# Landing numbers read ahead, and running counts per tile of tokens: one change to a fused attention and expert kernel

## The reference, cut to what matters

```python
logits = flat @ router_w.T
probs = jax.nn.softmax(logits.astype(jnp.float32), axis=-1)
topk_p, topk_i = jax.lax.top_k(probs, TOP_K)          # TOP_K = 2
topk_w = topk_p / jnp.maximum(topk_p.sum(-1, keepdims=True), 1e-09)
combine = combine.at[jnp.arange(T)[:, None], topk_i].add(topk_w)
for e in range(E):
    out = out + _mlp(flat, w_fc[e], w_proj[e]) * combine[:, e:e + 1]
out = out + _mlp(flat, shared_fc, shared_proj)
...
x = _layernorm(x + _L0_ffn_ref(x, ...), axis=-1)
```

## Time and profile before

| what | us |
|---|---|
| median of 3 runs (480.43 to 483.86) | 480.66 |
| the profiled execution | 480.25 |
| its span, first to last instruction | 478.4 |
| TensorE matmul busy | 443.9 (93%) |
| VectorE busy | 356.6 (75%) |
| ScalarE busy | 354.9 (74%) |
| GpSimd busy | 318.1 (66%) |

### The profile page before, as it was taken

The page is one execution under the profiler, slowest core; times in us unless marked ns, Lnnn a source line. Parts: engine busy times, 40 slices in busy tenths (PEclk is TensorE's granted clock), DMA queues, the critical chain, the costliest instruction groups (busy, mean ns, idle before and its releaser), DMA issues.

```text
span 478.4 us, 7874 instructions
## 1 busy us (share of the span) xinstructions
PE 443.9 (93%) x2193; PEld 288.9 (60%) x2193; DVE 356.6 (75%) x870; ACT 354.9 (74%) x557; POOL 318.1 (66%) x294
## 2 busy tenths in 40 slices
PE   8997999999999998877889988999999999999973
PEld 5343444444344333334666766789999999999821
DVE  5889999999999999999888977453333333555465
ACT  3989999999999999952675555556666666666655
POOL 4763788888898989881677667734555545655541
PEclk9998999999999999999999999999999999999999
DMA  8032226673434343200111111142223221222457
GB/s 284 11 93 84 78 73 214 217 245 136 157 136 159 136 157 136 92 1 1 47 45 52 50 41 52 55 111 59 69 68 85 67 65 53 62 70 66 147 176 220
DMA packets 41196, 48.68 MB, mean 102 GB/s; under 512 B 5616, under 2 KB 25266, under 8 KB 41152
## 3 DMA queue, kind: packets, MB, share of 16 engines
q1 hardware_dynamic: 35792, 39.16, 25.0%
q0 software_dynamic: 5216, 8.70, 6.0%
q10 hardware_dynamic: 144, 0.31, 0.3%
HBM read 19.26 MB, written 29.11 MB: 101 GB/s over the span
## 4 chain that ended last, share of the span: by engine, by line
PE 43%; POOL 22%; DVE 17%; issue 8%; ACT 6%; SPq 2%; DMA 2%; POOLq 0%; DVEq 0%; ACTq 0%
POOL memory_feat L505 17%; PE routed_ph L1591 13%; PE routed_po L1606 13%; PE dispatch_spo L1074 3%; PE dispatch_sph L1064 3%; DVE memory_y_raw L788 2%; POOL memory_feat L513 2%; DVE memory_prod L779 2%; POOL memory_prod L528 2%; PE routed_px L1579 2%; PE memory_nsum L630 2%; SPq L1737 1%; DVE memory_feat L779 1%; PE memory_ph L636 1%; DVE dispatch_stats L1319 1%
## 5 line engine op out<-in xcount | busy, mean ns | idle before, releaser
L505 POOL TENSOR_TENSOR memory_feat<-memory_feat,memory_p_tok 128x1024 f32<-128x1024 f32 x64 | 125.9, 2063 | 17.1 <-ACT memory_feat L400 14.2
L630 PE MATMUL memory_nsum<-memory_feat,tri 128*128 128x512 f32 x256 | 116.8, 598 | 6.3 <-ACT memory_last_rows L413 2.4
L1567 POOL DMA_INDIRECT pick_scratch<-routed_ob,routed_xg x71 | 72.1, 1016 | 65.2 <-DVE routed_ob L1689 52.0
L630 PEld LDWEIGHTS memory_nsum<-memory_feat,tri 128*128 128x128 f32 x256 | 47.6, 191 | 64.4 <-issue 54.6
L1274 POOL DMA_INDIRECT table_scratch<-dispatch_xrow,dispatch_slot x64 | 62.3, 973 | 30.3 <-issue 14.4
L1639 ACT ACTIVATE routed_rel<-routed_ph 128x512 f32<-128x512 f32 x71 | 42.3, 597 | 45.0 <-PE routed_ph L1591 45.0
L1689 DVE TENSOR_SCALAR routed_ob<-routed_po,routed_xg 128x128 f32<-128x128 f32 x71 | 22.6, 348 | 67.2 <-PE routed_po L1606 67.1
L1606 PE MATMUL routed_po<-routed_w2c,routed_hid 128*128 128x128 f32 x568 | 71.1, 275 | 0.5 <-ACT routed_hid L1648 0.5
L1591 PE MATMUL routed_ph<-routed_xs,routed_w1c 128*128 128x256 f32 (+1 forms) x368 | 71.2, 337 | 0.0
L779 DVE TENSOR_TENSOR memory_prod<-memory_nsum,memory_query 128x1024 f32<-128x1024 f32 x58 | 68.8, 1216 | 2.0 <-PE memory_nsum L630 1.8
L1606 PEld LDWEIGHTS routed_po<-routed_w2c,routed_hid 128*128 128x128 f32 x568 | 67.0, 192 | 0.8 <-ACT routed_hid L1648 0.7
(11 more groups left out here) (202 smaller groups left out, 695.6 us busy)
## 6 DMA issues: line engine op xcount, KB each, us to landing
table_scratch<-memory_blank SPq DMA_DIRECT2D x68, 260.0 KB, 2.6
dispatch_xrow<-pick_scratch SPq DMA_DIRECT2D x16, 256.0 KB, 3.1
routed_xg<-table_scratch SPq DMA_DIRECT2D x25, 130.0 KB, 2.2
w<-w_up SPq DMA_DIRECT2D x9, 256.0 KB, 2.7
w<-w_down SPq DMA_DIRECT2D x9, 256.0 KB, 3.2
x_tok<-x SPq DMA_DIRECT2D x4, 512.0 KB, 3.7
out<-x_tok SPq DMA_DIRECT2D x7, 256.0 KB, 4.1
routed_xg<-table_scratch SPq DMA_DIRECT2D x21, 65.0 KB, 1.9
```

Of the source, the lines that this page charges most:

```text
L505: nc.gpsimd.tensor_tensor(v, v, pv, ALU.mult).then_inc(wfeat_done, 1)
L630: last = nc.tensor.matmul(nsum[:, o:o + 512], tri[:], feat[:, i % U, h, q * 512:(q + 1) * 512], start=True, stop=True)
L1567: nc.gpsimd.indirect_dma_start(out=pick_dram, in_=ob[:, u, h, :], in_offset=None, out_offset=bass.IndirectOffsetOnAxis(ap=xg[:, t % XU, h, ...
```

## The change: what it does

Three edits. First, the reads of the landing numbers move: SP's routed loop reads the four numbers of group `t - 10` behind the load of tile `t`, for tiles 10 to 17, keeps all 32 in registers and hands them to the finish; the wait for `settled` moves with them, into tile 10. Second, `count` no longer reduces a group to one sum. It runs behind `choose` and in front of `place`, and adds the four tiles of `sel` one after another, so that `seen` holds the counts ahead of each of the 32 tiles; VectorE waits for the last of them. Third, `rank` makes two products, the triangular one and one with ones on the four rows of `seen`; it waits for its own group's count, where before it needed only the count of the group before. `totals` takes every fourth row of `seen`.

```diff
-        self.part = sb("part", [P, E])
-        self.seen = sb("seen", [P, NG + 1, E], F32R)
+        self.seen = sb("seen", [P, NT + 1, E], F32R)
...
             def rank(g):
                 pe.wait_ge(sel_done, g + 1)
-                pe.wait_ge(seen_done, g + 1)
+                pe.wait_ge(seen_done, g + 2)
                 pe.wait_ge(log_kept, g + 1)
-                sv = sel[:, g % 2].rearrange("p t e -> p (t e)")
-                nc.tensor.matmul(pr[:, 0:GT * E], tri_r[:], sv, start=True, stop=False)
-                for t in range(GT - 1):
-                    nc.tensor.matmul(pr[:, (t + 1) * E:GT * E], ones_r[:],
-                                     sel[:, g % 2, t:t + 1, :].broadcast_to([P, GT - 1 - t, E]), start=False, stop=False)
-                nc.tensor.matmul(pr[:, 0:GT * E], ones_r[:],
-                                 seen[:, g].unsqueeze(1).broadcast_to([P, GT, E]), start=False, stop=True
+                nc.tensor.matmul(pr, tri_r[:], sel[:, g % 2].rearrange("p t e -> p (t e)"), start=True, stop=False)
+                nc.tensor.matmul(pr, ones_r[:], seen[:, group(g), :].rearrange("p t e -> p (t e)"), start=False, stop=True
                                  ).then_inc(rank_done, 1)
...
-                nc.tensor.matmul(p_sum, ones_r[:], seen[:, 1:NG + 1].rearrange("p g e -> p (g e)"), start=True, stop=True
+                nc.tensor.matmul(p_sum, ones_r[:], seen[:, GT:NT + 1:GT, :], start=True, stop=True
...
             def count(g):
                 dve.wait_ge(sel_done, g + 1)
-                link(nc.vector.tensor_reduce(part[:], sel[:, g % 2].bitcast(F32).rearrange("p t e -> p e t"), AX.X,
-                                             ALU.add))
-                nc.vector.tensor_tensor(seen[:, g + 1], seen[:, g].bitcast(F32), part[:], ALU.add
-                                        ).then_inc(seen_done, 1)
+                for t in range(GT):
+                    n = g * GT + t
+                    last = nc.vector.tensor_tensor(seen[:, n + 1], seen[:, n].bitcast(F32), sel[:, g % 2, t].bitcast(F32),
+                                                   ALU.add)
+                    if t < GT - 1:
+                        link(last)
+                last.then_inc(seen_done, 1)
+                dve.wait_ge(seen_done, g + 2)
...
                     choose(0)
+                    count(0)
...
                 place(0)
-                count(0)
                 normalise(1)
                 residual(2)
                 choose(1)
+                count(1)
                 normalise(2)
                 place(1)
-                count(1)
                 reduce(NT - 3)
                 for g in range(1, NG - 1):
                     choose(g + 1)
+                    count(g + 1)
                     if g + 2 < NG:
                         residual(g + 2)
                     place(g + 1)
-                    count(g + 1)
...
+            due = []
+
+            def body(t, u):
+                load(t, u)
+                g = t - ASK_AT
+                if g == 0:
+                    sp.wait_ge(dis.settled, 1)
+                if 0 <= g < NG:
+                    due.append([sp.value_load(settle[g:g + 1, n:n + 1], min_val=16, max_val=32 * TILES) for n in range(U)])
+            tiles(lambda: None, body)
+            return due
...
-        def sync(sp):
-            sp.wait_ge(dis.settled, 1)
-
+        def sync(sp, due):
             def load(g):
-                due = [sp.value_load(settle[g:g + 1, u:u + 1], min_val=16, max_val=32 * TILES) for u in range(U)]
                 for u in range(U):
-                    sp.wait_ge(rou.scattered[u], due[u])
+                    sp.wait_ge(rou.scattered[u], due[g][u])
```

More of the change, by code:

```diff
@@ L98, in build @@
         late = Late(nc, c, early.xrow, x_tok)
-        rou = routed(nc, c, dis, ident, w1, w2, expert, start, needs, table, pick_dram)
-        fin = finish(nc, c, late, dis, rou, ident, y_all, eps, warm, settle, pick_dram, out)
+        rou = routed(nc, c, dis, ident, w1, w2, expert, start, needs, settle, table, pick_dram)
+        fin = finish(nc, c, late, rou, ident, y_all, eps, warm, pick_dram, out)
         block = c.enter_context(nc.Block())
@@ L106, in _ @@
             mem.background(sp, dis.sync)
-            rou.sync(sp)
-            fin.sync(sp)
+            due = rou.sync(sp)
+            fin.sync(sp, due)
         @block.scalar
@@ L880, in dispatch @@
         off, lg, best, which, gap = early.off, early.lg, early.best, early.which, early.gap
-        ratio, hot, sel, part, seen, base = early.ratio, early.hot, early.sel, early.part, early.seen, early.base
+        ratio, hot, sel, seen, base = early.ratio, early.hot, early.sel, early.seen, early.base
         hit, spot, slot = early.hit, early.spot, early.slot
@@ L1480, in dispatch, with routed @@
                              grouped=grouped, tabled=tabled, experts_in=experts_in, added=added, settled=settled)
-def routed(nc, outer, dis, ident, w1, w2, expert, start, needs, table, pick_dram):
+def routed(nc, outer, dis, ident, w1, w2, expert, start, needs, settle, table, pick_dram):
     HALVES = ROWS // P
@@ L1487, in routed @@
     XU = 8
+    ASK_AT = 10
     with ExitStack() as c:
@@ L1560, in load @@
                              ).then_inc(loaded[t % XU], 16)
-            tiles(lambda: None, load)
+            due = []
[8 more added lines that the diff above has]
+            return due
         def gpsimd(pool):
@@ L1696, in routed, with finish @@
                            x_kept=x_kept, rel_done=rel_done, banks=parts(TILES), kept=kept)
-def finish(nc, outer, late, dis, rou, ident, y_all, eps, warm, settle, pick_dram, out):
+def finish(nc, outer, late, rou, ident, y_all, eps, warm, pick_dram, out):
     with ExitStack() as c:
```

## The result

The changed kernel takes 488.66 us (median of 4 runs, 487.84 to 491.36) against 481.03 of the kernel before on the same chip (480.43 to 483.86): ratio 1.0162, 95% interval 1.0129 to 1.0196. The forecast was 480.9, with a range from 477.5 to 483.5; it was slower by 1.6% instead.

A forecast was written before the change was run, and what follows sets the result against it. SyncE's reads and load issues were taken to pace the finish from group 4 to 6, the rank to touch dispatch's chain. Span 478.4 + 4.7 - 4.4 = 478.7, execution 480.55, median forecast 480.9 us; range 477.5 to 483.5.

The forecast's parts named there:

- The finish term, -4.4: Finish: with the reads moved, loads leave early and VectorE and ScalarE set the pace; saves 4.4 us, bounds 3.6 to 5.0.
- rival 2: Finish: GpSimd's back-to-back additions hold off VectorE's shift; by all, +5.2 and 486.2 us, chance 0.05; by one more, 483.6, 0.08.
- the dispatch term: Dispatch: counts on VectorE delay the ranks, less the products saved; costs 4.7 us, bounds 3.5 to 5.4.
- Rival 1: Dispatch: TensorE is late anyway, so counts cost nothing: 476.3 us; covered or half covered 0.13, with 0.34 us saved too 0.03.
- Rival 3: Finish: loads issued all at once fill the DMA queues, last scatters land late; half the gain lost, 483 us, chance 0.05.

The follow-up runs named there:

- the reading ahead alone: The kernel before with only the reads of the landing numbers moved into SP's routed loop, dispatch unchanged: 481.82 us, ratio 0.9998.
- the change with the shift from PSUM: The whole change, with the shift's second input put into PSUM for the finish's first three groups: 483.32 us, ratio 1.0057 against the kernel before.
- the five products: The kernel before with the change's counts on VectorE, but ranks of five products waiting only for the previous group's count; reads not moved: 490.92 us, ratio 1.0204.
- the eight products: The kernel before with each group's three products for the ranks within it issued a second time, output the same: 482.38 us, ratio 1.0033.
- the two kernels with the freed shift: Kernel before with reads moved, and the whole change, each with the shift's second input in PSUM for three groups: 476.40 us and 483.32 us.
- the shift by tile: The kernel before with the reads moved and each shift made of four instructions, one per tile, with one SBUF tensor each: 479.22 us, ratio 0.9955.

## Why the prediction was wrong

**The finish term, -4.4, was the step that failed.** All its parts but one came as written: loads out early, no reads of `settle` at the end, no 1.20 us wait ahead of a group's statistics, ScalarE without a gap from group 2 on. What failed is the choice that "a shift waits for the addition under way, at most 1.3 us, and the sum above stands". The shift waited for all the additions that stood in line: rival 2 at its full price, 5.15 us measured against 5.2 worked out, at a chance of 0.05 (the finish, which that rival had 0.8 us longer than before, came out 0.4 shorter). Its mechanism is shown and not only argued: the stall is there with the reading ahead alone, gone without the additions, gone with one SBUF tensor, and gone with the second input in PSUM, beside the same additions. The term itself was sound under its condition: with the shift freed the finish is 5.4 us shorter, a little past the bound of 5.0. On what contends the Trainium skill (SBUF — State Buffer, Who interferes with whom) says that a VectorE instruction with two SBUF inputs contends with a GpSimd instruction that reads SBUF, and all four runs agree (5.15 us in the one with both, 0.16 to 0.58 in the others). That whoever is first keeps the ports for the whole instruction it says of VectorE's two-port modes, and the prediction carried it over to the shift. Who comes next when both have one waiting it doesn't say; here it was GpSimd, four times in a row.

The evidence that misled was the earlier trace rows: there every shift that met an addition ended with it, because before the change there never was a second addition waiting. The change itself closed the gaps between them. The prediction named this ("The trace holds no shift against two additions in a row") and still gave the forecast thirteen times the chance of the full hold-off.

This step isn't the whole miss. With the shift freed the whole change takes 483.32 us, still 2.4 above the forecast and at the edge of its range; that rest is the dispatch term, too small, and the clock.

**The dispatch term, +4.7, was right in mechanism and too small.** Without a fall of the clock it is 5.5 us, against an upper bound of 5.4. Rank 0 is late by 0.96 (0.91 forecast). Rank 3 is late by 3.35 in all, where the forecast has 1.82 + 0.4 and the 0.78 of its own count, 3.0. The last four ranks add 0.49 + 0.69 + 0.49 + 0.81 = 2.48, where it has 4 x 0.44 + 0.3 = 2.1. Behind the last rank 0.36 comes back, the three products saved (0.34). (From rank to rank in the change's profile; rank 0 to rank 1 from the change with the shift from PSUM, where the clock stood at 1.00.) The sum prices the wait of a rank from group 3 on; group 2's rank pays one, too: rank 1 to rank 2 is 0.94 longer with the five products and 1.39 with the two. Toward group 3 little is absorbed: the five products, which add no wait, have 0.54 of the 0.60 there, where 0.4 was taken. And the 0.34 us saved was taken off in full at each of five ranks; the nearest measurement, the eight products, shows about half of three products' time.

**The clock was in no sum.** 1.66 us of the profiled execution are the fall at 226 to 232; 5.5 + 1.66 makes the 7.13 of the table. The mean clocks of whole runs can't say how often such a fall comes: they also hold a fall near 44 us, in nine of the twelve profiles, and one behind TensorE's last product, in the change from 476 us to the end. So it stays open how much of the 6.9 us between the two kernels with the freed shift is the clock; in their profiles it is one fall, about 1.6. That waiting causes the falls was not shown: the shift by tile has the same two falls with before's dispatch.

**Rival 1**, the counts covered, is out: 6.9 us. **Rival 3**, late loads, is there in part: 0.8 us in the reading ahead alone (a scatter awaited 1.73 us; the last `ob` waits 1.44 to 1.94 for one in three of the kernels built on it, too), nothing in the change's own profile. The tile loads 11 to 18 made nobody wait: routed took 136.96 us against 136.97.

## What to carry to other kernels

When a change makes an engine's work denser, ask of each instruction that this engine was seen to hold off what it does against a full queue; a trace in which that engine had gaps can't answer. Here a small instruction with two SBUF inputs on the path was freed by putting one input into PSUM, and the early transfers were worth nothing until that was done. And a count moved from a side product of TensorE to chained sums on VectorE cost its whole length at three of five ranks (0.95 to 1.12 us for sums of 0.92) and little at the two others (0.02 and 0.28): read, group by group, who is late before calling the products saved a gain.

## What the runs showed of the hardware

- A VectorE instruction of 0.16 us with two SBUF inputs took 5.15 us, to 0.04 us behind the last of five GpSimd additions that followed each other without a gap, though it had come when the first was nearly over (464.31, with the additions from 463.27 at 1.23 us each). With one tensor in SBUF and a number per row as operand, or with the second input in PSUM, it wasn't held (0.58 for four, 0.16 for one).
- TensorE's granted clock fell to the lower level for some microseconds in dispatch, in six of the six profiles with sums on VectorE and in one of the six others; such a fall cost 1.30 to 1.67 us on the path where two profiles give its price, the one at 214 to 218 nothing (rank 0 at 19.45 with and without it). What brings it about stays open.
